# Attention and quantised feed-forward on one core: activation scales, normalising, the second quantiser's engine and all five orders changed

## The chip, the cores and the metric

The kernel runs on one core of a Trainium2 chip. The metric is the device time of one execution in microseconds; the time before is the median of three runs. The engines are TensorE (PE; PEld is its weight load), VectorE (DVE), ScalarE (ACT), GpSimd (POOL) and SyncE (SP), whose queue issues most DMAs. Each works through its own list of instructions in order and waits on semaphores for the others.

## The reference

One layer of cross attention with the 32 best keys of 1601, and one feed-forward part with quantised activations and ternary weights, for 2048 rows of 256 values:

```python
x = x + xattn(layernorm(x), ctx_1024, 32, Wq, bq, Wk, bk, Wv, bv, Wo, bo)
x = x + ffn(layernorm(x), w1, b1, w2, b2)

# xattn: scores = q @ k.T / 16; all but the 32 largest of a row are -inf; softmax; @ v; @ Wo.T + bo
def act_quant(x):
    scale = 127.0 / clip(max(abs(x), axis=-1), 1e-05)
    return clip(round(x * scale), -128, 127) / scale
def weight_quant(w):
    scale = 1.0 / clip(mean(abs(w)), 1e-05)
    return clip(round(w * scale), -1, 1) / scale
def bitlinear(x, w, b):                 # rmsnorm(x) = x * rsqrt(mean(x*x) + 1e-5)
    return act_quant(rmsnorm(x)) @ weight_quant(w).T + b
def ffn(x, w1, b1, w2, b2):             # 256 -> 1024 -> 256
    return bitlinear(gelu(bitlinear(x, w1, b1)), w2, b2)
```

## The kernel before

The 2048 rows are 16 tiles of 128 rows, two to a pair. The start turns the context, folds the query and key weights, makes keys and values in two parts of reduced precision (`high`, `low`), and makes the ternary weights. Then each tile t passes these steps, each named by a function with the engine in brackets:

- `ln1_stats` [DVE], `normalise_scale` and `normalise` [POOL], `turn_queries` [PE], `take_queries` [ACT], `split_queries` [POOL], for a pair j.
- `scores(t, c)` [PE] for four chunks c of about 400 keys, `copy_scores` [ACT] to `s_sb`, `candidates(t, c)` [DVE]: the 8 largest of each piece of 50.
- `best_8`, `next_8`, `count` [DVE] find the 32nd largest; `exp_all` [ACT]; `weigh` [DVE] zeroes in `e_all` what is below it. `turn_counts` [SP] brings the counts into one row, `largest_count` and `release` [DVE] branch on them and raise `p_ready`.
- `turn_weights(t, q)` [PE], `take_weights` [ACT], `weighted(t, q)` [PE] for four groups q; `residual` [POOL]; `attended` [DVE] makes x2; `moments` and `centre` [DVE] give its variance, the centred row and its maximum.
- `row_scales_1`, `quantise_1` [POOL], `turn_y1` [PE], `take_y1` [ACT], `up(t, h)` [PE] for two halves h, `hidden` [ACT], `add_bias` [POOL], `gelu`, `squares` [ACT], `gelu_max` [DVE].
- `row_scales_2` [POOL], `quantise_2` and `lower_2` [ACT], `turn_y2` [SP, a transposing DMA], `down` [PE], `keep_residual` [POOL], `output` [DVE], `store` [SP].

Rounding is by adding and subtracting `MAGIC` (12582912). In both scale functions on POOL seven tiny operations on 128x2 follow one another, each waiting for the last: mean square, its power -1/2, the product with the maximum, the step size, its reciprocal, the scale (step 5), and the factor of the product (step 6). In the last four tiles (12 to 15) the bias and parts of the second quantising go to DVE (`hidden`, `quantise_half`, `take_y2`), y2 is turned by TensorE, and tiles 14 and 15 have their scales one by one on DVE (`tile_spread_1`, `tile_scales`, `tile_spread_2`), with only the root on POOL (`root_1`, `root_2`). `hold_clock(23)` is 23 transposes with no use for the result.

The order of each engine is written by hand, as a list of calls at the end of its block, with a loop over rounds r in the middle: a round works on pairs r + 1, r, r - 1 and r - 2 in different steps. PSUM is eight banks, which `fill` gives out among a group and takes back by `drained`; `wait_full` and `wait_drained` are the waits that come with it.

## Time and profile before

| | us |
|---|---|
| median of 3 runs (lowest, highest) | 279.48 (278.39, 279.64) |
| the profiled execution, first to last instruction | 277.2 |
| TensorE busy | 262.5 (95%) |
| VectorE busy | 230.2 (83%) |
| ScalarE busy | 215.8 (78%) |
| GpSimd busy | 165.0 (60%) |
| mean granted TensorE clock | 0.999 |

The profiled execution's own time is known as its span alone, and the median of the runs lies 2.25 us above it. Busy time counts every moment in which at least one instruction of the engine runs, and matmul ends are modelled, so a busy TensorE can still have room. A wait is the idle time of an engine before an instruction, put down to the instruction that released it.

### The profile page before, as it was taken

The page shows a single profiled execution, that of the slowest core. Times are in us where ns is not written, and L with a number is a line of the kernel's source. Part 1 is how long each engine was busy: PE and PEld are TensorE (multiplying, and loading weights), DVE is VectorE, ACT ScalarE, POOL GpSimd, SP SyncE. Part 2 cuts the span into 40 slices and gives each one's busy share as a digit, 9 for nine tenths or more (in the row PEclk, how much of TensorE's full clock was granted, in tenths as well). Part 3 has the DMA queues.
Part 4 walks back from the last instruction along what each step waited for, and adds up shares of the span by engine and source line. Part 5 has one row for each costly group of instructions (what it writes and reads, how often), then busy time and mean ns, then how long its engine had stood idle before and what let it go on. Part 6 is the DMA issues. An engine that isn't in the chain of part 4 may idle for free. (4 is left out here: it accounts for less than half of the span.)

```text
span 277.2 us, 5366 instructions
## 1 busy us (share of the span) xinstructions
PE 262.5 (95%) x1527; PEld 230.4 (83%) x1527; DVE 230.2 (83%) x984; ACT 215.8 (78%) x323; POOL 165.0 (60%) x235
## 2 busy tenths in 40 slices
PE   7999999999999899999999999999999999799784
PEld 7999998998887788988898889888978898577463
DVE  2561868988979897989898989899989798989894
ACT  2567495586589988988799879987998899647762
POOL 3334409931888587849775887678767943612330
PEclk9999999999999999999999999999999999999999
DMA  6991010046000330025001500151004100610011
GB/s 223 316 342 40 4 38 0 1 79 151 2 2 0 77 78 0 0 69 125 0 4 45 139 5 4 38 140 18 0 1 124 31 1 2 151 38 5 0 38 38
DMA packets 29436, 16.42 MB, mean 59 GB/s; under 512 B 20445, under 2 KB 28190, under 8 KB 29406
## 3 DMA queue, kind: packets, MB, share of 16 engines
q1 hardware_dynamic: 28702, 15.02, 20.3%
q0 software_dynamic: 272, 0.79, 1.0%
q10 hardware_dynamic: 432, 0.26, 0.3%
q8 instruction: 12, 0.20, 0.3%
q14 instruction: 18, 0.15, 0.2%
HBM read 9.77 MB, written 2.10 MB: 43 GB/s over the span
## 5 line engine op out<-in xcount | busy, mean ns | idle before, releaser
L399 PE MATMUL bank<-vo,pT 128*128 128x257 f32 (+1 forms) x416 | 97.1, 381 | 2.4 <-ACT pT L1101 2.4
L399 PEld LDWEIGHTS bank<-vo,pT 128*128 128x128 f32 (+1 forms) x416 | 76.0, 190 | 15.1 <-ACT pT L1101 4.8
L1413 DVE MAX8 cand<-s_sb 128x8 f32<-128x50 f32 (+1 forms) x512 | 60.0, 201 | 1.6 <-issue 1.1
L258 PE MATMUL score<-k_high,q_low 128*128 128x400 f32 (+1 forms) x128 | 49.5, 387 | 0.0
L868 POOL TENSOR_TENSOR g<-g,b_bc 128x512 f32<-128x512 f32 x24 | 37.9, 1592 | 12.1 <-ACT g L1125 12.1
L258 PE MATMUL score<-k_low,q_high 128*128 128x400 f32 (+1 forms) x128 | 44.2, 346 | 0.0
L258 PE MATMUL score<-k_high,q_high 128*128 128x400 f32 (+1 forms) x128 | 44.0, 344 | 0.0
L1052 ACT ACTIVATE s_sb<-score 128x400 f32<-128x400 f32 x64 | 30.6, 504 | 10.2 <-PE score L258 10.1
L1101 ACT ACTIVATE pT<-bank 128x512 f32<-128x512 f32 x64 | 31.9, 514 | 4.2 <-PE bank L266 4.2
L1448 DVE SCALAR_TENSOR_TENSOR e_all<-s_sb,best,e_all 128x1601 f32<-128x1601 f32 x16 | 34.2, 2138 | 0.9 <-ACT e_all L1093 0.5
L266 PE MATMUL bank<-ident,e_all 128*128 128x128 f32 (+1 forms) x208 | 30.7, 273 | 2.6 <-ACT pT L1101 2.6
L1093 ACT ACTIVATE e_all<-s_sb,neg_max 128x1601 f32<-128x1601 f32 x16 | 26.1, 1629 | 4.5 <-DVE neg_max L1426 4.5
L266 PEld LDWEIGHTS bank<-ident,e_all 128*128 128x128 f32 (+1 forms) x208 | 24.4, 140 | 5.6 <-issue 3.6
L764 POOL TENSOR_SCALAR xn<-x_in,ln_mv,ln_r 128x256 f32<-128x256 f32 x16 | 27.8, 1741 | 0.9
L258 PEld LDWEIGHTS score<-k_high,q_low 128*128 128x128 f32 x128 | 24.1, 189 | 2.4
L258 PEld LDWEIGHTS score<-k_low,q_high 128*128 128x128 f32 x128 | 24.2, 189 | 0.7
L258 PEld LDWEIGHTS score<-k_high,q_high 128*128 128x128 f32 x128 | 24.1, 189 | 0.0
L1609 DVE TENSOR_REDUCE g_max<-g 128x1 f32<-128x1024 f32 x14 | 17.0, 1218 | 7.6 <-ACT g L1135 7.6
L1423 DVE MAX8 best<-cand 128x8 f32<-128x64 f32 (+1 forms) x64 | 20.8, 325 | 2.0
L822 POOL TENSOR_SCALAR row<-ln_mv 128x2 f32<-128x2 f32 x7 | 1.3, 192 | 28.8 <-issue 15.4
L1135 ACT ACTIVATE g<-g 128x1024 f32<-128x1024 f32 x14 | 14.9, 1067 | 3.7 <-POOL g L868 3.7
L1125 ACT ACTIVATE g<-bank,row 128x512 f32<-128x512 f32 x24 | 15.8, 685 | 2.3 <-PE bank L430 2.1
(162 smaller groups left out, 503.2 us busy)
## 6 DMA issues: line engine op xcount, KB each, us to landing
x_in<-in_x SPq DMA_DIRECT2D x16, 128.0 KB, 2.2
w_sb<-in_L_ffn_w SPq DMA_DIRECT2D x2, 1024.0 KB, 12.1
x_res<-in_x SPq DMA_DIRECT2D x16, 128.0 KB, 2.9
out<-o_sb SPq DMA_DIRECT2D x16, 128.0 KB, 2.0
ctx_sb<-in_ctx SPq DMA_DIRECT2D x2, 512.0 KB, 7.6
ctx_sb<-in_ctx SPq DMA_DIRECT2D x2, 256.0 KB, 4.1
b_bc<-in_L_ffn_b POOLq DMA_DIRECT2D x1, 512.0 KB, 7.6
w_q<-in_L_xattn_Wq SPq DMA_DIRECT2D x1, 256.0 KB, 2.8
```

The costliest lines, as they stand in the source:

```text
L258: ins = pe.matmul(out, a, b, start=(i == 0), stop=(i == len(steps) - 1))
L266: ins = pe.transpose(bank[0:src.shape[1], at:at + rows], src, ident[0:rows, 0:rows])
L399: ins = pe.matmul(bank[:, 0:DV], pT[0:n, t % 2, b * P:(b + 1) * P], vo[0:n, b, :], start=(b == 0), stop=(b == SB - 1))
L764: pool.tensor_scalar(xn[:, u, :], x_in[:, u, :], ln1_mv[:, u, 0:1], ln1_r[:, 1, u:u + 1], ALU.subtract, ALU.mult).then_inc(xn_ready, 1)
L868: pool.tensor_tensor(g[:, t % 2, part], g[:, t % 2, part], b1_bc[:, part], ALU.add).then_inc(biased, 1)
L1052: act.activation(s_sb[:, t % 2, at:at + n], score[c][:, 0:n], ACT.Copy).then_inc(s_copied, 1)
L1093: act.activation(e_all[:, t % 2, :], s_sb[:, t % 2, :], ACT.Exp, bias=neg_max[:, t % 2:t % 2 + 1], scale=SCALE).then_inc(e_ready, 1)
L1101: drain(act.activation(pT[0:rows, t % 2, lo * P:hi * P], bank(("p", t, q))[0:rows, 0:(hi - lo) * P], ACT.Copy), ("p", t, q))
L1413: ins = dve.max(cand[:, t % 2, k:CAND:PIECES], s_sb[:, t % 2, k * PIECE:end])
L1423: dve.max(best[:, u, k, :], cand[:, u, 0:DEPTH[k] * PIECES]).then_inc(topk_step[u], 1)
L1448: dve.scalar_tensor_tensor(e_all[:, u, :], s_sb[:, u, :], least_kept(t), e_all[:, u, :], ALU.is_ge, ALU.mult).then_inc(masked, 1)
L1609: dve.tensor_reduce(g_max[:, t % 2:t % 2 + 1], g[:, t % 2, :], AX.X, ALU.max, apply_absolute_value=True).then_inc(g_max_ready, 1)
```

## The change

- **Scales from the maxima alone.** Both activation scales are 127 over the largest value, in which the root mean square cancels. `scales_1` and `scales_2` make the step size from the maximum of the unnormalised row and its reciprocal, two operations; the clips become `CLIP1` and `CLIP2`. `quantise_1` and `quantise_2` need these two only. `dequant_1` and `dequant_2` make mean square, root and the factor of the product in four operations later on; they replace the rest of `row_scales_1` and `row_scales_2`. The same is done for tiles 14 and 15 on DVE (`tile_scales_1/2`, `tile_spread_1/2`, `tile_dequant_1/2`).
- **x normalised by add and multiply.** `normalise_scale` also makes the negated mean, and `normalise` adds it, where it subtracted the mean. Tiny operations with one function get a second one (times 1.0 or plus 0.0).
- **`quantise_2` and `lower_2` move from ACT to POOL**, as `tensor_scalar` over 1024 columns.
- **Orders.** All five lists of calls are written anew, without loops.

```diff
-ROW1, ROW2, X2S = 7, 7, 5
+ROW1, ROW2, X2S = 6, 6, 5
+CLIP1, CLIP2 = 1e-5 * EPS, 1e-5 * EPS ** 0.5
...
-                pool.tensor_scalar(xn[:, u, :], x_in[:, u, :], ln1_mv[:, u, 0:1], ln1_r[:, 1, u:u + 1],
-                                   ALU.subtract, ALU.mult).then_inc(xn_ready, 1)
+                pool.tensor_scalar(xn[:, u, :], x_in[:, u, :], ln1_r[:, 2, u:u + 1], ln1_r[:, 1, u:u + 1],
+                                   ALU.add, ALU.mult).then_inc(xn_ready, 1)
...
+            def quantise_2(t):
+
+                j = t // 2
+                pool.wait_ge(row2_step, j * ROW2 + 2)
+                if t >= 2:
+                    pool.wait_ge(y2_lowered, t - 1)
+                pool.tensor_scalar(y2_raised[:, t % 2, :], g[:, t % 2, :], row2[:, j % 2, 1, t % 2:t % 2 + 1], MAGIC,
+                                   ALU.mult, ALU.add).then_inc(y2_ready, 1)
+
+            def lower_2(t):
+
+                u = t % 2
+                pool.wait_ge(y2_ready, t + 1)
+                if t >= 2:
+                    pool.wait_ge(y2_turned[u], t // 2 * 16)
+                pool.tensor_scalar(y2[:, u, :], y2_raised[:, u, :], -MAGIC, 1.0, ALU.add, ALU.mult).then_inc(y2_lowered, 1)
...
+                pool.tensor_scalar(row1[:, v, 0, :], cen_max[:, pair], CLIP1, 1.0 / 127.0, ALU.max,
+                                   ALU.mult).then_inc(row1_step, 1)
+                pool.wait_ge(row1_step, base + 1)
+                pool.tensor_tensor(row1[:, v, 1, :], row1[:, v, 0, :], minus_one[:, :], ALU.pow).then_inc(row1_step, 1)
...
                 if t >= 2:
                     act.wait_ge(y2_ready, t - 1)
+                    act.wait_ge(g_sq_ready, t - 1)
...
-            def quantise_2(t):
-
-                j = t // 2
-                act.wait_ge(row2_step, j * ROW2 + 6)
-                if t >= 2:
-                    act.wait_ge(y2_lowered, t - 1)
-                act.activation(y2_raised[:, t % 2, :], g[:, t % 2, :], ACT.Identity, scale=row2[:, j % 2, 5, t % 2:t % 2 + 1],
-                               bias=magic_col[:, 0:1]).then_inc(y2_ready, 1)
...
             down(12)
-            up(15, 0)
-            up(15, 1)
             down(13)
-            hold_clock(23)
             turn_y2(14, 0)
...
             turn_y2(15, 0)
             turn_y2(15, 1)
-            down(14)
             down(15)
+            hold_clock(23)
```

The new orders, where the prediction speaks of them:

- DVE: `ln1_stats(0)` after `leave_context(2)`; `weight_means`, `candidates(0, 0)`, `ln1_stats(2)` before `leave_keys(3, *)`; then the rest of tile 0's candidates, its top-k, `weigh(0)`, `candidates(1, 0)`, (1, 1), `largest_count(0)`, `ln1_stats(3)`, `candidates(1, 2)`, `release(0)`, `candidates(1, 3)`. `attended(0)` after `weigh(2)`; `gelu_max(0)` and (1) amid the candidates of tile 5. After `release(15)`: `attended(14)`, `output(10)`, `moments(14)`, `hidden(12, *)`, `centre(14)`, scales and `quantise_1(14)`, `hidden(13, *)`, `gelu_max(12)`, (13), `output(11)`, `hidden(14, *)`, a maximum, `attended(15)`, ..., `quantise_1(15)`.
- PE: `scores(0, 0)`, (0, 1) after `project_keys(2, 1)`, then keys (3, *) with `weight_mean` between, one value block, the other scores of tile 0, scores of tile 1, the other values. In the tail `up(12)`, `up(13)` go between the turned weights of tile 15, `up(14)` into its weighted sums.
- ACT: `sum_weights(0)` after `take_keys(2, 0)`, `sum_weights(1)` before `copy_scores(0, 0)`.
- POOL: in each pair `scales_2`, `quantise_2`, `lower_2` of both tiles, then `scales_1` and `quantise_1` of the next pair, then `dequant_2`, `dequant_1`, `add_bias`.
- SP: `load_x(2)`, (3), (4) before `turn_counts(0)`, (1), (2).

## Rows read from the trace of the kernel before

**Rows 1.** Chain that ended last: start us, us, engine and line.

```profile
206.14 1.11 PE score L258 x6
207.24 0.87 PE bank L266 x8
208.12 0.87 PE bank L454 x8
209.86 3.48 PE bank L399 x16
...
216.08 0.45 PE bank L430 x2
```

**Rows 2.** Windows: length, busy us (count) per engine, PE clock, DMA share, GB/s.

```profile
47.28:247.10 199.82, 194.10 (x1094) 168.59 (x1093) 179.63 (x804) 168.78 (x245) 139.43 (x191) 1.00 0.20 46
...
124.47:152.61 28.14, 27.63 (x158) 23.90 (x156) 25.87 (x115) 25.35 (x37) 21.23 (x29) 1.00 0.19 46
...
266.00:272.00 6.00, 4.00 (x35) 3.50 (x34) 5.41 (x19) 4.04 (x7) 2.73 (x4) 1.00 0.08 25
```

**Rows 3.** Instructions of line 1448: ns minimum, median, maximum.

```profile
L1448 DVE SCALAR_TENSOR_TENSOR e_all<-s_sb,best,e_all x16: 1876/1886/2977, 37.2 to 244.2; 128x1601 f32<-128x1601 f32 x16
```

**Rows 4.** Timeline of DVE, the start: start us, us, [idle before, releaser].

```profile
27.86 0.64 DVE L1393 SCALAR_TENSOR_TENSOR k_low<-bank,k_bias,k_high 128x401 fp32r<-128x401 f32 x1 [5.18 <-ACT k_high L1033]
...
41.25 0.16 DVE L1404 TENSOR_SCALAR wmean<-bank 128x2 f32<-128x2 f32 x1 [1.66 <-PE bank L378]
...
42.80 3.69 DVE L1413 MAX8 cand<-s_sb 128x8 f32<-128x50 f32 x32 [1.13 <-issue]
...
47.28 0.19 DVE L1423 MAX8 best<-cand 128x8 f32<-128x64 f32 x1
```

**Rows 5.** Waits of DVE from 47.28 to 247.1: us, times, longest.

```profile
DVE g_max L1609 <- ACT g L1135: 7.6, 6, 1.9
DVE inv_sum L1497 <- PE bank L399: 5.1, 7, 1.0
```

**Rows 6.** Groups of DVE, 47.28 to 247.1 (mean ns), and timelines in tile 7.

```profile
L1448 DVE SCALAR_TENSOR_TENSOR e_all<-s_sb,best,e_all 128x1601 f32<-128x1601 f32 x15 | 32.3, 2155 | 0.9 <-ACT e_all L1093 0.5
...
L1455 DVE SCALAR_TENSOR_TENSOR cand_ge<-cand,best,cand_worth 128x256 bf16<-128x256 f32 x15 | 8.2, 545 | 0.5
...
132.97 2.97 DVE L1448 SCALAR_TENSOR_TENSOR e_all<-s_sb,best,e_all 128x1601 f32<-128x1601 f32 x1
...
132.99 1.27 POOL L868 TENSOR_TENSOR g<-g,b_bc 128x512 f32<-128x512 f32 x1 [0.91 <-ACT g L1125]
134.68 3.67 POOL L868 TENSOR_TENSOR g<-g,b_bc 128x512 f32<-128x512 f32 x2 [0.42 <-ACT g L1125]
```

**Rows 7.** Groups by shape, ACT: busy us, mean ns, idle before.

```profile
L1161 ACT ACTIVATE y_raised<-g,magic_col,row 128x1024 f32<-128x1024 f32 x14 | 17.3, 1242 | 0.2 <-POOL row L890 0.2
...
L1179 ACT ACTIVATE y<-y_raised,unmagic_col 128x1024 bf16<-128x1024 f32 x12 | 13.8, 1150 | 0.2
```

**Rows 8.** Groups by shape, POOL: busy us, mean ns, idle before.

```profile
L764 POOL TENSOR_SCALAR xn<-x_in,ln_mv,ln_r 128x256 f32<-128x256 f32 x16 | 27.8, 1741 | 0.9
...
L835 POOL TENSOR_SCALAR y<-cen,row 128x256 f32<-128x256 f32 x14 | 6.5, 479 | 0.7
...
L795 POOL TENSOR_SCALAR w_sb<-w_sb,winv 128x2048 f32<-128x2048 f32 x2 | 3.9, 1970 | 8.7 <-DVE winv L1406 8.7
```

**Rows 9.** Timelines of DVE and ACT in the tail.

```profile
246.63 0.26 DVE L1462 TENSOR_REDUCE doubtful<-counts_row 1x1 int32<-1x128 f32 x1
...
261.68 0.34 DVE L1556 TENSOR_SCALAR y<-cen,row 128x256 f32<-128x256 f32 x1
...
264.71 1.40 DVE L1584 SCALAR_TENSOR_TENSOR s_sb<-score,row,b_bc 128x512 f32<-128x512 f32 x2
...
270.48 0.82 ACT L1170 ACTIVATE y_raised<-s_sb,magic_col,row 128x512 f32<-128x512 f32 x1 [1.77 <-DVE row L1533]
...
274.51 0.48 DVE L1632 SCALAR_TENSOR_TENSOR o_sb<-score,row,x2b 128x256 f32<-128x256 f32 x1 [0.58 <-PE score L454]
```

More of the change, by code:

```diff
@@ L1729, in _ @@
[L1729 to L1730 removed]
+            candidates(1, 3)
+            best_8(1, 0)
+            next_8(1, 1)
+            next_8(1, 2)
+            next_8(1, 3)
+            count(1)
+            weigh(1)
+            largest_count(1)
+            candidates(2, 0)
+            release(1)
+            candidates(2, 1)
+            candidates(2, 2)
+            candidates(2, 3)
+            best_8(2, 0)
+            candidates(3, 0)
+            candidates(3, 1)
+            candidates(3, 2)
@@ new lines, in _ @@
+            gelu_max(0)
+            gelu_max(1)
+            candidates(5, 3)
+            best_8(5, 0)
+            attended(3)
+            centre(2)
+            next_8(5, 1)
+            moments(3)
+            next_8(5, 2)
+            centre(3)
+            next_8(5, 3)
+            count(5)
+            weigh(5)
+            largest_count(5)
+            attended(4)
+            release(5)
+            output(0)
+            moments(4)
+            candidates(6, 0)
+            candidates(6, 1)
@@ new lines, in _ @@
+            candidates(6, 2)
+            candidates(6, 3)
+            best_8(6, 0)
+            next_8(6, 1)
+            next_8(6, 2)
+            ln1_stats(5)
+            next_8(6, 3)
+            candidates(7, 0)
+            count(6)
+            gelu_max(2)
+            gelu_max(3)
+            output(1)
+            largest_count(6)
+            weigh(6)
+            release(6)
+            candidates(7, 1)
+            candidates(7, 2)
+            centre(4)
+            attended(5)
+            candidates(7, 3)
@@ new lines, in _ @@
+            centre(6)
+            next_8(8, 3)
+            gelu_max(4)
+            count(8)
+            output(2)
+            gelu_max(5)
+            candidates(9, 0)
+            ln1_stats(7)
+            weigh(8)
+            largest_count(8)
+            output(3)
+            release(8)
+            candidates(9, 1)
+            attended(7)
+            moments(7)
+            centre(7)
+            candidates(9, 2)
+            candidates(9, 3)
+            candidates(10, 0)
+            best_8(9, 0)
```

1386 lines of the change are left out of this document (900 added, 486 removed).

## The prediction, made before the changed kernel was timed

> **What bounds the kernel now.** I read the views in this order: the spacing of the matmuls in the chain, busy time by window, the timelines of the start, the waits of the vector engine (DVE), its groups, POOL beside it, the tail. The page has TensorE busy for 95% of the span, yet that is overlap, since ends are modelled: in the chain 16 matmuls of weights times values take 3.48 us, six of a score chunk 1.11, eight transposes 0.87, the eight of `down` 0.87, two of `up` 0.45 [rows 1]. A tile has 4 score chunks (4.44), 13 transposes (1.41), 13 weighted matmuls (2.83), 4 `up` (0.90), 8 `down` (0.87) and some 4 small turns (0.44): 10.9 us, 21.8 for a pair. A steady pair takes 28.14 us [rows 2], so TensorE has over 6 us of slack in it. In that window DVE is busy 25.87 us, ACT 25.35, POOL 21.23 [rows 2]. DVE's remainder is 1.4 us of named waits and 0.9 us of small gaps. DVE is the bound, ACT stands close behind, and part of DVE's busy time isn't work: `weigh` (L1448, the masking of `e_all`) takes 1.886 us at the median and up to 2.977 [rows 3].
>
> I cut DVE's time in three: until the first pick of the eight best of tile 1 (47.28 us [rows 4]); from there to the end of `largest_count(15)`, 246.63 + 0.26 = 246.9 us [rows 9], which frees the last tile's weights; and the tail to 277.2 us, 30.3 us long.
>
> **Part one, the start.** DVE stood idle 5.18 us before the keys (3, 0) while ACT took queries, values and the sum of w1; it waited 1.66 us for `weight_means` and 1.13 us after `release(0)` [rows 4]. The new orders put `ln1_stats(0)` some steps earlier, `scores(0, 0)` and (0, 1) ahead of the keys (3, *) and the first values, `weight_means` and `ln1_stats(2)` into the former gap, and candidates of tile 1 around `release(0)`. Stepped through with the present durations: ACT finishes keys (2, 0) near 20.5, both sums of weights and what stands between by 26.1, and copies score chunk (0, 0) by 26.6. TensorE issues without a pause here and only changes its order; chunk (0, 3) comes about 30.4, its candidates end near 32 against 34.1. Top-k of tile 0 (3.1) and `weigh(0)` (1.9) bring 37.0; tile 1's candidates (3.7), the largest count (0.3), `ln1_stats(3)` (0.94) and `release(0)` (0.4) bring the first pick of tile 1 to 42.3: 5.0 us earlier, with 0.94 us done ahead. I allow 41.5 to 44. On SP, `load_x(2)`, (3), (4) now stand ahead of `turn_counts(0)`, (1), (2), each waiting on `xn_ready`; the normalising they wait for lies over 5 us ahead of the count, so I cost them at nothing. Without that cover `largest_count` would wait, and `release` and the turned weights behind it.
>
> **Part two, the middle.** It lasted 246.9 - 47.28 = 199.6 us. Off it come:
> - the named waits, 7.6 (maxima after GELU) + 5.1 (`attended` after `weighted`) = 12.7 us [rows 5];
> - DVE standing behind POOL, 15 x (2.155 - 1.886) = 4.0 us of `weigh` and, by its undisturbed 0.48, 15 x (0.545 - 0.48) = 1.0 us of `count` [rows 3, 6];
> - work done elsewhere: ln1 of pair 3 (0.94), outputs 10 and 11 (0.95) and `hidden(12, 0)` (0.74), the last three now in the tail.
>
> That leaves 179.3 us. *Waits that return.* ACT loses `quantise_2` (1.24 us) in fourteen tiles and `lower_2` (1.15 us) in twelve [rows 7], 4.8 us of 25.35 in a pair. It relieves the engine that stands in front of both waits, but takes nothing off DVE. The orders also give slack: `attended(0)` stood after `count(1)`, now after `weigh(2)`; the maxima of tiles 0 and 1 stood in tile 4, now in tile 5. The last tiles keep less lag. I let 4 us of 12.7 return; 1 and 11 are the ends. The waits that are added (`hidden` for the squares, `lower_2` for the transposed y2) name things done a tile earlier: nothing. If `lower_2` did wait, `scales_1` and `quantise_1`, so y1, would be queued behind it on POOL.
>
> *POOL's own time.* `normalise` took 1.74 us at the mean for 256 columns with subtract and multiply, where `quantise_1` with multiply and add takes 0.479 for as many; multiply and add on 2048 columns take 1.97 us [rows 8]. A line through the two is 0.27 us + 0.83 ns a column. For add and multiply no row exists: the ends are 0.48 and the 1.23 us of an undisturbed `normalise`. I take 0.48, because it is the fast row's pair of operations in the other order; below that nothing is to be gained, since the time would be under the line of the fast form. The new operations of 1024 columns then cost 1.12 us each. A pair: 21.23 - 3.1 (x) - 0.4 (two small operations less in each of two sets, an estimate) + 0.2 (the negated mean) + 4.5 = 22.4 us of about 27. It fits into POOL's idle time and costs nothing by itself; without that cover y1 slips with it.
>
> *Standing behind POOL.* In tile 7 `weigh` starts at 132.97 and takes 2.97 us; POOL's add, started at 132.99, takes its plain 1.27; the next adds start within `weigh`, and two take 3.67 instead of 2.54 [rows 6]. DVE waited 1.08 us for the first, POOL for DVE after that. With POOL busier, and operations of 1.1 us where there was idle time, more starts of `weigh`, `count` and the centring meet one. From 5.0 us I go to 9.0; the ends are 5 (nothing changes) and 13 (15 x 0.87, near the worst row's 1.08 for every tile).
>
> The Trainium skill, SBUF — State Buffer, section Who interferes with whom, says that the ports which VectorE shares with GpSimd are locked for a whole instruction and that the order of issue decides who blocks; a VectorE operation with two SBUF inputs takes part. By that rule, the trace agrees (1.08 us of the add's 1.27), and it speaks against this change: if all 30 `weigh` and `count` met half an add, the term would be 19 us, and the time 276.
>
> Middle: 179.3 + 4 + 9 = 192.3 us; the last tile is released at 42.3 + 192.3 = 234.6 us.
>
> **Part three, the tail.** y1(15) was done at 262.0, hidden(15) began at 264.71, ACT's half of the quantising at 270.48, the last output ended at 274.99 [rows 9]. Between GELU (266.8) and 270.48 lay the squares, mean square, POOL's root, the maximum and four small steps. Scales need only the maxima now; three small steps of about 0.18 us remain. Stepping the new orders from the release R: ACT ends `gelu(12)` at R + 5.4; y1(14) is taken at 7.8, weighted(15) done at 9.9, `attended(15)` at 11.8, y1(15) at 17.2, since hidden (13) and (14), their maxima and two outputs stand before it; then 2.2 to hidden(15), 1.4, 0.65 GELU, 0.68 maximum, 0.55 scales, and `squares(15)` still ahead of ACT's half until 22.7, quantising 0.8, turn 0.6, taking 0.8, `down` 1.0, output 0.5: R + 26.4, and 2.2 for the store, 28.6. I take 29.0, against 30.3 with 1.7 us less work in it; ends 26.5 and 31. `hold_clock(23)` moves behind the last `down`: 23 x 0.109 = 2.5 us under the output and store (2.7), at no cost, and it no longer holds the clock for anything.
>
> **Sum.** 42.3 + 192.3 + 29.0 = 263.6 us of span. The median of the runs shown, 279.48, is 2.25 above the profiled span of 277.23; with the same addition the forecast is 266 us, 5% less.
>
> **Rivals.**
> - *DVE is fed throughout.* Locks stay at 5, 1 us of waits returns, tail 27: 42.3 + 179.3 + 6 + 27 + 2.25 = 257 us. For it: ACT is no longer near the bound. Against it: POOL is busier.
> - *The gain is handed back between DVE and POOL.* Locks 13, waits 9, start 43, tail 29: 43 + 179.3 + 22 + 29 + 2.25 = 275.5 us, 273 at half the excess. For it: quantising and lowering stand ahead of `scales_1` and `quantise_1` in POOL's queue, so a late maximum delays the next y1, and the locks as read above.
> - *Slower: add and multiply is no fast form on POOL.* A column then costs (1.23 - 0.27)/256 = 3.7 ns, `lower_2` 4.1 us, and `normalise` stays. POOL's 139.4 us of the middle [rows 2] are, by the forecast, 27 more (24 x 1.12), 19 less for x, 6 less for scales and for a ternary step that goes ahead: 141. Here come 35 + 6 on top, and some 15 blocked behind DVE: 197, more than DVE's 192. From 4 us a lowering POOL is the bound; its bursts of 10 us make y1 and GELU late, 10 us of waits come back, R is 250, and with a tail of 31 the time is 283 us.
> - *The clock falls in the tail*, with the hold gone. 266:272 was granted 1.00 [rows 2], 2.4 GHz. At 1.2 GHz the last turns, `up` and `down`, about 2.6 us of the path, double: 268.5 us, in the forecast's own range.
>
> **How the numbers follow.** Forecast, 261 to 269.5: 0.53, the clock case within. Fed throughout, 254 to 261: 0.20. Handed back, 269.5 to 278: 0.18. Slow POOL form: 0.06. Another cause of slower: 0.03. The range, 256 to 275, leaves out 0.06 below and 0.14 above. A measurement of this kernel tells some 0.5% from no change (278.1 to 280.9). Faster by more: 0.53 + 0.20 + 0.16 = 0.89; within: 0.04; slower: 0.07.
>
> **What would show it.** `normalise` at 0.5 us and POOL's operations on `y_raised` and `y` at 1.1; ACT under 190 us busy; first pick of tile 1 near 42 us; DVE's named waits in the middle near 4 us; `weigh` at a mean over 2.2 us; the last release near 235 us and 29 us behind it. Wrong would be a pair that still takes 28 us, POOL over 85% busy, or `lower_2` at 4 us.

## The result and the profile after

| | before | after |
|---|---|---|
| median of the runs, us | 279.39 | 283.49 (281.81 to 285.84) |
| ratio, 95% interval | | 1.0165 (1.0109 to 1.0220) |
| profiled execution's own time, us | | 282.66 |
| its span, us | 277.2 | 280.9 |

The change makes the kernel 1.65% slower. The forecast was 266.0 us, 5% faster. The busy times on the page of the changed kernel:

```profile
PE 262.0 (93%) x1527; PEld 230.1 (82%) x1527; DVE 232.4 (83%) x978; ACT 188.3 (67%) x297; POOL 182.5 (65%) x255
```

ACT lost 27.5 us of work and POOL gained 17.5, as planned, while VectorE's busy time didn't fall but rose by 2.2 us. The best way to see where the time went is to cut both executions at the same pieces of work. I take the first `best_8` of tiles 1, 8 and 14, and ask for busy time by window. First the kernel before, then the changed one (length, busy us and count per engine, clock, DMA share, GB/s):

```profile
47.28:142.20 94.92, 92.48 (x514) 80.91 (x513) 84.18 (x390) 77.17 (x113) 67.60 (x86) 1.00 0.19 43
142.20:226.10 83.90, 82.71 (x474) 72.24 (x473) 75.89 (x339) 76.07 (x112) 63.02 (x86) 1.00 0.19 45
226.10:277.20 51.10, 41.60 (x257) 33.03 (x255) 42.55 (x137) 34.52 (x51) 15.31 (x33) 1.00 0.14 37
```

```profile
42.71:142.60 99.89, 93.75 (x528) 81.79 (x527) 83.91 (x387) 65.35 (x105) 62.43 (x86) 1.00 0.18 39
142.60:226.50 83.90, 81.98 (x468) 71.88 (x466) 76.47 (x335) 61.43 (x98) 67.37 (x88) 1.00 0.20 44
226.50:280.90 54.40, 46.07 (x282) 37.40 (x280) 43.39 (x133) 34.24 (x52) 30.02 (x42) 0.97 0.13 34
```

The start is 4.6 us shorter. The stretch to tile 8 is 5.0 us longer, and with that the whole gain of the start is gone. Three pairs in the steady state take 83.9 us in both kernels, to the tenth, although ScalarE (ACT) has 14.6 us less to do in them. The end is 3.3 us longer. -4.6 + 5.0 + 0 + 3.3 = +3.7 us, the difference of the spans. In the stretch to tile 8, VectorE works 84 us in both kernels and is idle 16.0 us instead of 10.7.

VectorE's waits between 42.71 and 248.74 us (us, times, longest), which answer to [rows 5]:

```profile
DVE cand L1743 <- ACT s_sb L1293: 7.5, 8, 2.0
DVE inv_sum L1827 <- PE bank L400: 6.3, 7, 1.4
DVE o_sb L1976 <- POOL row L1071: 2.9, 1, 2.9
DVE cand L1743 <- issue: 1.0, 2, 0.6
DVE cand L1743 <- DVE doubtful L1792: 1.0, 1, 1.0
DVE g_max L1953 <- ACT g L1379: 1.0, 2, 0.7
```

With three smaller ones they add up to 21.0 us. The wait for GELU went from 7.6 to 1.0 us. In its place VectorE waits 7.5 us for scores, and 6.3 for weighted values. TensorE works through its list in order, and in this stretch it stood at `turn_y1` for POOL:

```profile
PE bank L267 <- POOL y L1015: 5.5, 4, 1.8
```

Scores that stand behind such a place in the list come later; that this is the whole reason for the 7.5 us is not shown (e1, below, took most of these waits away and was slower). Two of the four places, in TensorE's timeline (start, length, then in brackets the idle time before and its releaser):

```profile
78.13 0.66 PE L267 MATMUL bank<-ident,y 128*128 128x128 f32 x4 [1.62 <-POOL y L1015]
...
104.97 0.66 PE L267 MATMUL bank<-ident,y 128*128 128x128 f32 x4 [1.13 <-POOL y L1015]
```

Why y1 is late at 104.97 can be read in VectorE's and POOL's timelines:

```profile
101.24 2.88 DVE L1778 SCALAR_TENSOR_TENSOR e_all<-s_sb,best,e_all 128x1601 f32<-128x1601 f32 x1
```

```profile
101.14 1.30 POOL L926 TENSOR_TENSOR q_low<-q_full,q_high 128x512 fp32r<-128x512 f32 x1
102.53 2.39 POOL L1015 TENSOR_SCALAR y<-cen,row 128x256 f32<-128x256 f32 x2
```

`weigh` starts 0.1 us after POOL's subtraction and takes 2.88 us instead of 1.89; the two `quantise_1`, 0.48 us each when nothing stands in the way, are issued while it runs and end at 104.92, 0.8 us after `weigh` does. This is the lock of [rows 6], now with a third engine behind it: TensorE's 1.13 us.

A part of the loss is in the clock, and the profiled execution doesn't show all of it. The four executions of the changed kernel had mean granted clocks of 0.994, 0.994, 0.988 and 0.982, and spans of 280.9, 280.0, 282.5 and 284.0 us. The kernel before, measured beside the other runs, had 0.991 to 1.000 and 276.4 to 279.0. What one fall costs can be read where the same work ran with it and without: the changed kernel, and then a4, which differs from it in the tail alone. Both have the same 1.77 us of waiting for y1 in front of 136 us.

```profile
134.00:136.00 2.00, 0.28 (x3) 0.28 (x4) 1.97 (x7) 0.00 (x0) 2.00 (x3) 1.00 0.04 0
136.00:138.00 2.00, 2.00 (x14) 1.68 (x13) 1.93 (x11) 1.18 (x2) 1.65 (x5) 1.00 0.23 58
```

```profile
134.00:136.00 2.00, 0.23 (x2) 0.09 (x2) 2.00 (x6) 0.00 (x0) 2.00 (x3) 0.98 0.04 0
136.00:138.00 2.00, 2.00 (x8) 1.99 (x9) 1.89 (x12) 0.69 (x1) 1.65 (x5) 0.50 0.16 31
```

In a4 the clock fell to 0.50 there, the lower of its two levels (1.2 GHz, where 1.00 is 2.4 GHz), and from the pick of tile 7 to that of tile 8 it took 15.85 us instead of 14.27: 1.6 us. So a wait of TensorE for POOL can be paid twice, and the second time not in every execution.

### The profile page after: what moved, and what is told of

Same layout as the page of the kernel before. It is cut to its first block, busy times and chain, and to the rows that moved or that the text cites. A ratio compares the mean times of both kernels' runs of the same rounds, so it can differ in the third digit from the quotient of the medians.

```text
span 280.9 us, 5388 instructions
## 1 busy us (share of the span) xinstructions
PE 262.0 (93%) x1527; PEld 230.1 (82%) x1527; DVE 232.4 (83%) x978; ACT 188.3 (67%) x297; POOL 182.5 (65%) x255
## 4 chain that ended last, share of the span: by engine, by line
PE 46%; POOL 18%; DVE 17%; issue 10%; ACT 5%; DMA 3%; DVEq 1%; SPq 0%; POOLq 0%; ACTq 0%
PE score L259 13%; PE bank L400 12%; PE bank L259 7%; PE bank L267 6%; POOL y L1015 4%; POOL g L1048 3%; DVE cand L1743 3%; DMA ctx_sb<-in_ctx 3%; DVE g_max L1953 2%; PE bank L431 2%; POOL y_raised L964 2%; ACT g L1379 2%; POOL row L993 1%; DVE e_all L1778 1%; PE bank L455 1%
## 5 line engine op out<-in xcount | busy, mean ns | idle before, releaser
L1743 DVE MAX8 cand<-s_sb 128x8 f32<-128x50 f32 (+1 forms) x512 | 61.6, 202 | 9.9 <-ACT s_sb L1293 7.5
L1293 ACT ACTIVATE s_sb<-score 128x400 f32<-128x400 f32 x64 | 31.5, 505 | 17.0 <-PE score L259 16.6
L1048 POOL TENSOR_TENSOR g<-g,b_bc 128x512 f32<-128x512 f32 x24 | 35.3, 1476 | 8.4 <-ACT g L1369 8.3
L1778 DVE SCALAR_TENSOR_TENSOR e_all<-s_sb,best,e_all 128x1601 f32<-128x1601 f32 x16 | 33.8, 2115 | 0.0
L964 POOL TENSOR_SCALAR y_raised<-g,row 128x1024 f32<-128x1024 f32 x14 | 17.4, 1246 | 0.6
L926 POOL TENSOR_TENSOR q_low<-q_full,q_high 128x512 fp32r<-128x512 f32 x8 | 10.2, 1279 | 10.6 <-ACT q_full L1285 10.6
```

The source lines that it names most:

```text
L964: pool.tensor_scalar(y2_raised[:, t % 2, :], g[:, t % 2, :], row2[:, j % 2, 1, t % 2:t % 2 + 1], MAGIC, ALU.mult, ALU.add).then_inc(y2_rea ...
L1048: pool.tensor_tensor(g[:, t % 2, part], g[:, t % 2, part], b1_bc[:, part], ALU.add).then_inc(biased, 1)
L1293: act.activation(s_sb[:, t % 2, at:at + n], score[c][:, 0:n], ACT.Copy).then_inc(s_copied, 1)
L1743: ins = dve.max(cand[:, t % 2, k:CAND:PIECES], s_sb[:, t % 2, k * PIECE:end])
L1778: dve.scalar_tensor_tensor(e_all[:, u, :], s_sb[:, u, :], least_kept(t), e_all[:, u, :], ALU.is_ge, ALU.mult).then_inc(masked, 1)
```

## The experiments

All ratios are to the kernel before, measured on the same chip beside each run; 0.01 is 2.8 us. "Old orders" are the five lists of before, "new orders" those of the changed kernel.

| kernel | us | ratio (95%) |
|---|---|---|
| a1 old orders, new arithmetic | 284.36 | 1.0162 (1.0136 to 1.0188) |
| a2 old orders, quantising on ScalarE | 276.77 | 0.9882 (0.9858 to 0.9906) |
| a3 new orders, quantising on ScalarE | 314.21 | 1.1216 (1.1192 to 1.1240) |
| a4 changed kernel, holder moved | 282.56 | 1.0092 (1.0062 to 1.0122) |
| b1 new orders, POOL quantises 32 columns | 279.21 | 0.9978 (0.9956 to 0.9999) |
| b2 as a3, spread | 308.99 | 1.1034 (1.1010 to 1.1058) |
| b3 as a2, new start | 277.94 | 0.9923 (0.9899 to 0.9946) |
| b4 old orders, POOL quantises 32 columns | 276.79 | 0.9881 (0.9858 to 0.9904) |
| c1 before, two of three score products | 278.37 | 0.9961 (0.9938 to 0.9983) |
| c2 changed kernel, two of three | 283.41 | 1.0161 (1.0113 to 1.0209) |
| c3 as a2, two of three | 274.49 | 0.9835 (0.9797 to 0.9873) |
| c4 as b3, two of three | 274.91 | 0.9832 (0.9802 to 0.9863) |
| e1 changed kernel, later turns | 286.88 | 1.0268 (1.0239 to 1.0298) |
| e4 as a2, waits moved | 277.91 | 0.9947 (0.9924 to 0.9971) |
| e5 as e4, shorter tail | 277.58 | 0.9935 (0.9909 to 0.9962) |
| f1 as e4, two of three | 276.28 | 0.9895 (0.9852 to 0.9938) |
| f2 as b1, two of three | 278.34 | 0.9954 (0.9923 to 0.9985) |
| f3 as a2, shorter tail | 276.47 | 0.9891 (0.9848 to 0.9933) |

### The arithmetic and the orders apart: a1, a2, a3, b2

**a1** takes the changed kernel and puts the five lists of before under it, with the new calls at the places of the old:

```diff
-                    row_scales_2(r + 2)
+                    scales_2(r + 2)
+                    quantise_2(2 * r + 4)
+                    lower_2(2 * r + 4)
+                    quantise_2(2 * r + 5)
+                    lower_2(2 * r + 5)
+                    dequant_2(r + 2)
```

> All of the new arithmetic (scales from the maxima alone, x normalised by add and multiply, the second quantised activations and their lowering on GpSimd), under the five orders of the kernel before; the clock holder stands where it stood before. Theory O (the new orders cost the time: in the new order of TensorE the turns of y1 stand ahead of scores and come before GpSimd has them, and everything behind them slips): the first pick of tile 1 is back at 47 us, the middle from there to the last release falls below the 199.6 us of before, since g_max and the scales no longer wait for ScalarE, and the time is 270 to 278 us. Theory G (quantising and lowering on GpSimd, 2.4 us a tile, lengthens the way to y1 under any order, and the locks with VectorE add to it): the 5 us of the earlier start are lost and nothing comes back for them, 285 to 290 us.

**a2** leaves the quantising where it was:

```diff
-                pool.tensor_scalar(y2_raised[:, t % 2, :], g[:, t % 2, :], row2[:, j % 2, 1, t % 2:t % 2 + 1], MAGIC,
-                                   ALU.mult, ALU.add).then_inc(y2_ready, 1)
+                act.activation(y2_raised[:, t % 2, :], g[:, t % 2, :], ACT.Identity, scale=row2[:, j % 2, 1, t % 2:t % 2 + 1],
+                               bias=magic_col[:, 0:1]).then_inc(y2_ready, 1)
```

> The same, but the second activations are quantised and lowered by ScalarE, at their old places in its order; only the scales and the normalising are new. Theory O: 273 to 279 us, as the old orders hold the time whoever quantises; within 2 us of the kernel with old orders and quantising on GpSimd. Theory G: 275 to 279 us too, but that kernel is slower than this one by 6 us or more.

Measured 284.4 and 276.8 us. The new orders, taken whole, are worth nothing against the old ones under the new arithmetic (1.0165 and 1.0162), and the quantising on POOL costs 7.6 us under the old orders: theory G, whose difference was 6 us or more, though a1 itself lies just under its 285 us. The new scales and the new `normalise` gain 1.2%. Cut at the same picks, a1 takes 46.4 + 97.2 + 87.3 + 51.0 us and a2 47.3 + 94.0 + 83.8 + 49.8: most of the price of the POOL quantising falls before tile 14, 3.2 and 3.4 us. The groups of VectorE in a1 and then in a2 (busy us, mean ns) show what it consists of:

```profile
L1542 DVE TENSOR_SCALAR cen<-x,ln_mv 128x256 f32<-128x256 f32 x16 | 9.8, 615 | 0.3
L1483 DVE SCALAR_TENSOR_TENSOR cand_ge<-cand,best,cand_worth 128x256 bf16<-128x256 f32 x16 | 9.6, 598 | 0.5
...
L1651 DVE TENSOR_REDUCE g_max<-g 128x1 f32<-128x1024 f32 x14 | 17.0, 1218 | 10.1 <-ACT g L1193 10.1
```

```profile
L1537 DVE TENSOR_SCALAR cen<-x,ln_mv 128x256 f32<-128x256 f32 x16 | 5.5, 345 | 0.3
L1478 DVE SCALAR_TENSOR_TENSOR cand_ge<-cand,best,cand_worth 128x256 bf16<-128x256 f32 x16 | 8.0, 503 | 0.5
...
L1646 DVE TENSOR_REDUCE g_max<-g 128x1 f32<-128x1024 f32 x14 | 17.0, 1218 | 7.7 <-ACT g L1158 7.7
```

VectorE is busy 233.1 us in a1 and 227.7 in a2, 5.4 more. The centring has 4.3 us more and the count 1.6, standing behind POOL, and `weigh` 0.5 less; another 2.4 us are the longer wait for GELU. 5.4 + 2.4 = 7.8 us, against 7.0 us between the spans.

**a3** is the other half, the new orders with the quantising back on ScalarE, each pair ahead of the next `take_y1`; **b2** is the same with each pair where ScalarE had room in the trace of the changed kernel.

```diff
+            quantise_2(0)
+            lower_2(0)
+            quantise_2(1)
+            lower_2(1)
             take_y1(1)
```

> The changed kernel with its new orders, but the second activations quantised and lowered by ScalarE, the pair of them just ahead of the next take_y1 in ScalarE's order. Theory G: GpSimd reaches y1 2.4 us a tile earlier, TensorE no longer waits at the turns of y1, ScalarE has 26 us a run more to do but was busy 188 of 281 us: 274 to 279 us. Theory O: the waits stay, at other places, 282 to 288 us.

> New orders, quantising on ScalarE, but each pair placed where the trace of the changed kernel shows ScalarE idle or just done with the squares, some 15 us earlier than in the kernel of 314 us, where SyncE's turns of the activations stood ahead of the counts' and VectorE waited 26 us for them. If that queue was the whole of the 314 us: 276 to 282 us. If the new orders do not bear a later y2 at all: over 290 us. Faster than the changed kernel only if GpSimd's share (theory G) outweighs what ScalarE's 29 us push back.

Measured 314 and 309 us. Both theories missed for a3; of the two cases for b2 the one over 290 us came. VectorE's largest waits, a3 and then b2:

```profile
DVE doubtful L1792 <- DMA counts_row<-counts: 26.4, 6, 9.8
```

```profile
DVE doubtful L1792 <- DMA counts_row<-counts: 13.4, 4, 6.3
DVE cand L1743 <- ACT s_sb L1250: 13.0, 6, 4.5
```

SyncE's list has `turn_y2` of a pair ahead of `turn_counts`, so a late y2 keeps VectorE from its counts, and `release` with it. The new lists bear neither of these two placings on ScalarE. The two runs say nothing on what POOL's quantising costs under them; b1 does.

### What each engine's work is worth: b1, b4

Both leave out part of the result: POOL quantises and lowers 32 of 1024 columns of tiles 0 to 11.

```diff
-                pool.tensor_scalar(y2_raised[:, t % 2, :], g[:, t % 2, :], row2[:, j % 2, 1, t % 2:t % 2 + 1], MAGIC,
+                n = F if t >= LAST - 2 else 32
+                pool.tensor_scalar(y2_raised[:, t % 2, 0:n], g[:, t % 2, 0:n], row2[:, j % 2, 1, t % 2:t % 2 + 1], MAGIC,
```

> The changed kernel, in which GpSimd quantises and lowers only 32 of the 1024 columns of tiles 0 to 11; every instruction, wait and place stays (the rest of those columns isn't computed). It takes 12 x (1.12 + 1.04) us, less some 0.2 us each for the stubs, about 22 us of work off GpSimd, and nearly all of its locks with VectorE. Theory G (the length of this work on GpSimd and its locks cost the time): the middle falls from 206.0 us to 192 to 197, the whole to 269 to 275 us. Theory O (the new orders by themselves): 280 to 283 us, as only the locks, at most 4 us, go.

> Old orders with all of the new arithmetic (284.4 us), and the same stubs of 32 columns on GpSimd for tiles 0 to 11. Against the kernel with old orders and quantising on ScalarE (276.8 us) it has ScalarE's 29 us of quantising taken away and next to nothing put in its place: what that relief is worth by itself. Theory G1 (ScalarE stands in nobody's way): 276 to 277 us. Theory G2 (my forecast: the waits for ScalarE's gelu, 7.7 us in that kernel, fall with the relief): 269 to 273 us.

b4 has next to nothing of the quantising on any engine (the stubs, and tiles 12 and 13 on POOL) and takes 276.79 us; a2 has it on ScalarE and takes 276.77. **Relieving ScalarE of 28.7 us of work is worth nothing** in these orders, and the whole 7.6 us of a1 are POOL's doing. VectorE's waits for GELU and for the weighted values are the same in both, a2 first:

```profile
DVE g_max L1646 <- ACT g L1158: 7.7, 6, 1.9
DVE inv_sum L1520 <- PE bank L400: 5.1, 7, 1.0
```

```profile
DVE g_max L1652 <- ACT g L1194: 7.7, 6, 1.9
DVE inv_sum L1526 <- PE bank L400: 5.4, 7, 1.0
```

b1 is 1.9% below the changed kernel, 5.2 us by the ratios and 4.3 by the medians, with VectorE busy 228.4 instead of 232.4 us. It is between the theories: POOL's quantising costs 4 to 5 us under the new orders too, and what is left, 279.2 us, is 2.4 us slower than b4 in spite of the earlier start.

### The start by itself: b3

a2 with the head of the five lists from the changed kernel, up to the first pick of tile 1 (one of the moves):

```diff
-            project_keys(3, 0)
-            project_keys(3, 1)
             scores(0, 0)
             scores(0, 1)
+            project_keys(3, 0)
+            weight_mean()
+            project_keys(3, 1)
+            project_values(0)
             scores(0, 2)
```

> Old orders with quantising on ScalarE (276.8 us), and the start of all five lists laid as in the changed kernel, up to the first pick of tile 1. That pick moves from 47.3 to 42.7 us. If the start is a gain of its own: 271.5 to 273 us. If the middle gives it back (the rounds are paced by the chain through y1, gelu and y2, and not by VectorE's list): 275 to 277 us.

The pick of tile 1 comes at 42.09 us, 5.2 earlier, and the time is 1.2 us longer, above both ranges. VectorE's timeline shows the whole gain lost before the next tile, whose first pick came at 59.0 us in a2:

```profile
42.09 0.23 DVE L1753 MAX8 best<-cand 128x8 f32<-128x64 f32 x1
...
51.87 0.17 DVE L1827 RECIPROCAL inv_sum<-bank 128x1 f32<-128x1 f32 x1 [6.61 <-PE bank L400]
...
59.23 0.23 DVE L1753 MAX8 best<-cand 128x8 f32<-128x64 f32 x1
```

VectorE waits 6.61 us for the weighted sums of tile 0, which need every block of the projected values; those were put behind the scores to make the start shorter. TensorE had 40.3 us of work done at 42.1, against 45.7 at 47.3, so it owed 5 us. In the changed kernel the same debt is paid later: its picks of tiles 2 to 5 come at 52.4, 63.2, 75.1 and 94.5 us, against 59.0, 72.3, 85.6 and 100.4 before. It is 10.5 us ahead at tile 4 and 0.4 behind at tile 8 (142.6 against 142.2). Up to the pick of tile 4, before and then changed:

```profile
0.00:85.61 85.61, 83.64 (x495) 78.06 (x495) 61.52 (x283) 54.49 (x88) 43.67 (x59) 1.00 0.33 97
0.00:75.12 75.12, 72.59 (x442) 69.20 (x443) 57.00 (x280) 46.72 (x77) 30.71 (x55) 1.00 0.39 114
```

TensorE has 11 us less work done at that point, and VectorE 4.5: the lead is work put off. b3 leaves `attended(0)` at its old place, where the changed kernel moved it behind `weigh(2)`; the start together with that move alone was not run.

### Is TensorE the bound? c1 to c4

Each score chunk leaves out one of its three products, so the scores are less exact:

```diff
-                steps = [(a, b) for ah, al, bh, bl in factors for a, b in ((al, bh), (ah, bl), (ah, bh))]
+                steps = [(a, b) for ah, al, bh, bl in factors for a, b in ((al, bh), (ah, bl), (ah, bh))[first:]]
```

> The kernel before, with one of the three products of each score chunk left out (low queries by high keys), so that its scores are less exact: 64 x 2 matmuls of 0.185 us, 23.7 us of TensorE's work, some 21 of it behind the first pick of tile 1. Nothing of any other engine changes. Theory T (TensorE paces the middle: 26 matmuls of weights by values a tile, not 13, make 27.4 of the 28.14 us of a pair): the time falls until VectorE's 25.9 us of a pair are the bound, 1.5 to 2 us a pair, to 264 to 270 us. Theory D (VectorE is the bound and TensorE has 6 us of slack, as I forecast): 278 to 280 us.

> The changed kernel with the same product left out. Theory T: TensorE has room for its waits on GpSimd's y1 (5.5 us), and the start of 42.7 us counts: 264 to 274 us. Theory D: the 21 us of VectorE's waits in the middle come from GpSimd and the queues and stay, 280 to 284 us.

> Old orders, new scales and normalising, quantising on ScalarE (276.8 us), with the same product left out. Theory T: 262 to 268 us, 1 to 3 below the kernel before with that product left out, since VectorE is now next and has 1 to 2 us less of locks. Theory D: 275 to 277 us.

> The same with the start laid anew (277.9 us with all three products). Theory T: the start of 42.1 instead of 47.3 us was paid back by TensorE work that it put off (5.3 us); with TensorE relieved, VectorE's earlier start counts, and this kernel is 3 to 5 us faster than the one with the old start. Theory D: the same 0 to 1 us slower as with all products, the round's latency deciding.

Theory T falls. TensorE's busy time drops by 17.0 us in c1, 15.9 in c2 and 19.8 in c3. The kernel before gains 0.4%, the changed one nothing (1.0161 against 1.0165), and a2 1.3 us by the ratios, 2.3 by the medians and 3.1 by the mean spans, no more than the 3.3 us by which its first pick of tile 1 came earlier (44.0 us). c4 and c3 are equal, so the earlier start doesn't pay with a relieved TensorE either. Three steady pairs of c3, and VectorE's waits in them:

```profile
137.70:221.00 83.30, 75.29 (x426) 63.57 (x426) 75.26 (x338) 75.55 (x112) 52.79 (x82) 1.00 0.19 45
```

```profile
DVE g_max L1646 <- ACT g L1158: 3.2, 3, 1.9
DVE inv_sum L1520 <- PE bank L400: 2.1, 3, 0.7
```

TensorE works 7.7 us less than in a2's 83.8 us, and the pairs are 0.5 us shorter. The two waits, 3.2 and 2.1 us, are those of the kernel before in the same pairs. TensorE's own new idle time goes into waiting for ScalarE: 3.7 us for turned weights in these pairs, and in the whole of c1 the transposes of the weights wait 12.6 us for it where they waited 2.6. With less to do TensorE also had a lower clock (means of 0.981 to 0.994 in the executions of c1, against 0.991 to 1.000 in those of the kernel before), but that doesn't hide a gain: of c3's executions the one at 1.000 had a span of 272.1 us and those at 0.993 had 270.8 and 271.2.

### Places or latency: e1, e4, e5, f1, f2, f3

**e1** moves three `turn_y1` behind the work that follows them, and `dequant_2(0)` ahead of `scales_1(1)`:

```diff
             scores(6, 0)
-            turn_y1(1)
             down(0)
             scores(6, 1)
+            turn_y1(1)
```

> The changed kernel, with three turns of y1 put behind the work that follows them in TensorE's order (pairs 0, 1 and 2, where it stood 5.5 us for GpSimd in all), and dequant_2(0) ahead of scales_1(1) on GpSimd, since VectorE's first output stood 2.9 us for it. Theory P (the gain of the start is lost in the places where one engine's list stands for another's, between tiles 4 and 8): 277 to 280 us. Theory L (what comes late is the chain centring, scales, y1, up, GELU itself, which no place in a list shortens): 282.5 to 284 us, the waits reappearing behind up and GELU.

286.9 us, 1.0% slower than the changed kernel. TensorE's waits for y1 fell from 5.5 to 1.6 us, and VectorE then waited 4.4 us in one place for `down`, and TensorE 3.3 us for the low queries, behind which the granted clock was 0.50 from 106 to 108 us; in the profile of the changed kernel it was 1.00 there. Theory P is refuted for these moves, and the size of L as well: a step that is moved off one wait stands before another.

**e4** moves two steps of VectorE's list behind candidates:

```diff
-                if live(r - 1):
-                    gelu_max(2 * r - 2)
                 if live(r + 1):
                     candidates(2 * r + 2, 1)
+                if live(r - 1):
+                    gelu_max(2 * r - 2)
...
                 if live(r):
+                    candidates(2 * r + 3, 0)
                     attended(2 * r + 1)
```

> Old orders, new scales and normalising, quantising on ScalarE (276.8 us), with two moves in VectorE's list of each round: the first candidates of the next tile go ahead of attended, and those of the even tile ahead of the first maximum after GELU, about 1 us of work each. Its named waits in the middle are 7.7 (maxima) and 5.1 us (attended). Neither less work on TensorE nor on ScalarE shortened them. Theory P (they are a matter of the place in VectorE's list): they fall to under 4 us, and the time to 267 to 271 us. Theory L (a loop of fixed latency runs through them): the waits keep their sum within 3 us, at these places or others, and the time stays at 275.5 to 278 us.

277.9 us, 1.1 us slower than a2. The waits for GELU and the weighted values fell from 12.8 to 2.7 us, and 11.8 us of new ones stand before the candidates. In the three steady pairs:

```profile
DVE cand L1436 <- ACT s_sb L1072: 2.1, 2, 1.1
DVE g_max L1646 <- ACT g L1158: 1.9, 1, 1.9
DVE cand L1436 <- issue: 1.6, 3, 0.5
```

5.6 us, against 5.3 in c3 and in the kernel before. Of the 11.8 us, 8.2 are waits for ScalarE's copies of the scores. ScalarE was relieved in b4 alone, at the old places; e4 with ScalarE relieved was not run. **e5** is e4 with a shorter tail, and is compared with e4; **f3** is a2 with that tail alone. On ScalarE `squares(15)` goes behind its half of tile 14, and on VectorE:

```diff
             tile_scales_2(14)
+            quantise_half(14, 1)
             tile_spread_2(14)
-            output(13)
             gelu_max_half(15, 0)
             gelu_max_half(15, 1)
-            quantise_half(14, 1)
             tile_scales_2(15)
             quantise_half(15, 1)
-            tile_dequant_2(14)
+            output(13)
             tile_spread_2(15)
             take_y2(14, 1)
+            tile_dequant_2(14)
```

> The same kernel of 276.8 us with its tail laid so that nothing of tile 14 stands between the last GELU and the quantising of tile 15: scales_2(14) and both halves of its quantising ahead of the last maxima, output(13) behind the last quantising. Scales of tile 15 end 0.5 us and ScalarE's half starts 0.5 us earlier: 0.4 to 1.2 us faster if VectorE's steps set the end. No change if TensorE's turn of tile 14 behind the holder's matmuls does.

> The kernel of 276.8 us with the shorter tail alone. The run that was to show the tail carried the two moves of VectorE's list too, by my mistake; against the kernel with the moves alone it was 0.3 us faster, its last stretch 0.5 us shorter. Here 275.9 to 276.6 us; if the tail brings nothing, 276.8.

e5 is 0.3 us below e4 and f3 0.3 us below a2, both within their intervals. f3 is the lowest of the exact kernels by its median, 276.5 us, but not to be told from a2.

**f1** puts e4 and the left-out product together, **f2** b1 and the left-out product; their edits stand above.

> Old orders, new scales and normalising, quantising on ScalarE, the two moves in VectorE's list, and one of the three products of each score chunk left out (less exact scores, 23.7 us less for TensorE). Each by itself did little: the product left out gave 274.5 us against 276.8, with the 12.9 us of waits for GELU and the weighted values as before; the moves gave 277.9 us, with those waits turned into 8.2 us for copied scores. Theory B (two bounds at one height: VectorE's list with its waits, and TensorE's 27.4 us of a pair of 28.14; whoever is relieved alone meets the other): both together free the 10 us that neither did, 263 to 268 us. Theory L (a loop of fixed latency whatever the engines do): 273 to 276 us.

> The changed kernel with GpSimd quantising 32 of 1024 columns of tiles 0 to 11 (279.2 us with three products) and two of the three products of each score chunk. By itself the product left out gave 283.4 us against 283.5. Theory B for the new orders: with GpSimd and TensorE both relieved, VectorE's work of 228 us paces, 266 to 272 us. Theory L: the waits of the new orders stay (y1, released weights, low queries, each late for TensorE), 277 to 280 us.

Theory B falls as well: 276.3 and 278.3 us, the first just above the range of theory L. Three steady pairs of f1:

```profile
139.60:223.90 84.30, 76.83 (x426) 63.15 (x426) 77.46 (x339) 75.38 (x111) 52.53 (x82) 1.00 0.19 45
```

VectorE's waits there are 2.1, 1.6 and 0.7 us, 4.4 in all, but it is busy 77.5 us instead of 75.3 in c3: `weigh` takes 2306 ns at the mean over the kernel, against 2109 in c3, and `count` 619 against 526. What the moves took out of the waits came back as standing behind POOL. Three steady pairs last 83.3 to 84.4 us in before, changed kernel, a2, b4, c3, e4 and f1, with ScalarE at 61 or 76 us, TensorE at 75 to 83, and the waits at different places. Off this mark are a1 with 87.3 us and b1 with 82.0, where POOL's load under the same orders was changed, and a3 and b2 (97.6 and 94.0), where y2 came late.

Two explanations are left. One is a ring of dependences through all four engines. The other is VectorE's own list: it is busy 74 to 77 us of every such stretch, and what is left over is 8.0 us in before, 7.4 in the changed kernel, 8.1 in a2 and e4, 8.0 in c3 and 7.9 in b1 (6.8 in f1, 10.5 in a1). No run took work off VectorE, so none decides between the two, and which ring it would be is not shown either.

### The tail: a4

```diff
             down(14)
+            hold_clock(23)
             turn_y2(15, 0)
             turn_y2(15, 1)
             down(15)
-            hold_clock(23)
```

> The changed kernel, with the 23 matmuls that hold TensorE's clock moved from the end of its queue to between down(14) and the turn of the last activations. Both theories: they ran alone for 2.5 us after the last output and ended last, that tail goes; down(15) took 1.9 us at a granted clock of 0.56 to 0.59 and may now take 1.0: 1.3 to 3.5 us faster than the changed kernel, 279.5 to 282 us. If the holder delays the turn it stands before, the gain is under 1 us.

1.0092 against 1.0165: 0.7%, 2.0 us faster than the changed kernel by the ratios, a gain within the 1.3 to 3.5 us expected, though the time itself is above the range given. The two intervals together leave room for 0.3 to 3.8 us, and the medians differ by 0.9. Against a1 (1.0162, with a narrower interval) it is 0.7% too: the new orders with this holder are worth about 2 us over the old ones. Windows and TensorE's timeline in the tail of the changed kernel, and then the last `down` of a4:

```profile
270.00:273.00 3.00, 0.63 (x6) 0.32 (x4) 2.84 (x8) 2.68 (x5) 0.00 (x0) 1.00 0.00 0
273.00:275.00 2.00, 1.09 (x8) 0.86 (x8) 1.12 (x5) 1.19 (x2) 0.55 (x1) 1.00 0.19 66
275.00:277.00 2.00, 1.41 (x7) 1.02 (x8) 0.49 (x1) 0.04 (x1) 0.00 (x0) 0.56 0.03 8
277.00:279.00 2.00, 2.00 (x13) 1.96 (x11) 0.48 (x1) 0.00 (x0) 0.00 (x0) 0.59 0.02 8
```

```profile
275.59 1.86 PE L455 MATMUL score<-w2T,y2T 128*128 128x256 bf16 x8 [0.90 <-ACT y2T L1244]
277.25 3.36 PE L421 MATMUL bank<-ident 128*128 128x128 f32 x23
```

```profile
277.50 1.03 PE L455 MATMUL score<-w2T,y2T 128*128 128x256 bf16 x8 [0.90 <-ACT y2T L1244]
```

TensorE was busy 0.63 of 3 us, and the granted clock then fell to 0.56, that is to the lower level of 1.2 GHz for most of the window. The last `down` took 1.86 us instead of 1.03, and the holder, which now follows it, ran 3.36 us, until 280.61, 2.5 us behind the end of the last output (278.07). With the holder in the gap the clock is 1.00 there, and both prices go. They are smaller than they look. `down` gives back 0.8 us. The store of the last output takes as long as most of the holder: in a4 the output ends at 279.16 and the span at 281.4, 2.2 us later, and 278.07 + 2.2 = 280.3 against 280.9, so the holder itself costs 0.6. The profiled span of a4 is no shorter than that of the changed kernel because of the fall at 136 us; its one execution with a mean clock of 0.999 had a span of 279.3 us.

## Why the prediction was wrong, point by point

- **Part one** held: first pick of tile 1 at 42.71 us against 42.3. But it was booked as a gain of the whole. It is a loan: b3 and c4 show that an earlier pick is worth nothing with `attended(0)` at its old place, as the values that TensorE put off are owed to it, and in the changed kernel the lead of 10.5 us at tile 4 went with 11 us of TensorE's work put off.
- **TensorE's slack**, "over 6 us" in a pair, was a miscount. A tile has 26 records of `weighted` and not 13: 416 in 16 tiles, two for each of 13 blocks. 26 x 3.48 / 16 = 5.66 us instead of 2.83 [rows 1], which makes 13.7 us a tile and 27.4 of the 28.14 us of a pair. The page's 95% was right. A forecast of 263.6 us of span held 262.5 us of TensorE work and should have been stopped by that. The miscount was not the whole cause, though: with 17 to 20 us less work on TensorE (c1, c3), the forecast's gain still doesn't come.
- **The waits that return** are the step that failed most. 12.7 us of waits were taken off, because the engine in front of them was relieved and the orders gave slack, and 4 put back; 21.0 came. The middle took 206.0 us (42.71 to 248.74) and not 192.3, 13.7 more, and this term alone is 17.0 of it; with 21.0 and the 9.8 of the next point in it, the sum would be 210.1, and 4.1 us of small gaps and small steps went the other way. b4 shows the first reason to be void: with ScalarE relieved of the whole, the waits for GELU and for weighted values are the same to 0.3 us. So ScalarE's load did not set them; what does stays open. Subtracting named waits from a stretch is not a forecast, unless what releases them is shown to come earlier.
- **Standing behind POOL.** The forecast was 5 us before and 9 after; 9.8 came by the same reckoning: 3.7 us in `weigh` (2115 ns against 1886), 1.8 in `count`, and 4.3 in the centring, which I named as joining and gave no number. The total is right. In the middle VectorE's busy time rose less, from 179.6 to 180.2 us, as 2.6 us of its work went elsewhere by the forecast's own list. A faster `normalise` takes little of the standing away: in a2 `weigh` stays at 2114 ns against 2138, and `count` goes from 541 to 503, 1.0 us in all over the kernel. The forecast also took the locks as VectorE's cost alone; 101.24 to 104.97 us shows them reach TensorE through y1. By the Trainium skill, SBUF — State Buffer, section Who interferes with whom, a `tensor_scalar` of VectorE can take the shared port pair too, when it runs in a two-port mode; the trace agrees (the centring goes from 355 ns at most before to 1367 ns at most after), and this should have been in the sum.
- **Prices on POOL** were near: `quantise_2` 1.25 us at the mean, `lower_2` 1.16, with a forecast of 1.12; `normalise` 0.65 with the locks, forecast 0.48. The groups (busy us, mean ns, idle before):

```profile
L964 POOL TENSOR_SCALAR y_raised<-g,row 128x1024 f32<-128x1024 f32 x14 | 17.4, 1246 | 0.6
L973 POOL TENSOR_SCALAR y<-y_raised 128x1024 bf16<-128x1024 f32 x12 | 14.0, 1163 | 0.9
L1015 POOL TENSOR_SCALAR y<-cen,row 128x256 f32<-128x256 f32 x14 | 12.8, 922 | 0.7
...
L920 POOL TENSOR_SCALAR xn<-x_in,ln_r 128x256 f32<-128x256 f32 x16 | 10.3, 648 | 4.5 <-PE bank L267 4.3
```

  "It fits into POOL's idle time and costs nothing by itself" was the second step to fail: b1 puts the price at 4 to 5 us and a1 against b4 at 7.6, with POOL busy only 65% of the span. `quantise_1`, which makes y1, went from 0.48 to 0.92 us at the mean.
- **Part three**: 29.0 us forecast, 32.2 measured (248.74 to 280.9). `quantise_1(15)` was done 18.6 us after the release, hidden(15) began 20.5 after it and ScalarE's half 24.0, each 1.1 to 1.4 us later than stepped through. The holder "at no cost" and a clock that stays were wrong: 2.0 us by a4, of which the traces show 1.4. The rival on the clock had the mechanism for the tail and about the size, 2.6 us, but of other parts: `down` lost 0.8 us where turns, `up` and `down` were to lose 2.6, and it lacked the holder behind the last output and the falls in the middle.
- **The addition** of 2.25 us compares a median with the span of one execution. The changed kernel's profiled execution has 282.66 - 280.9 = 1.8; this is small beside the rest.
- **The rivals.** The slower one named a POOL form that proved fast. "Handed back between DVE and POOL" had the mechanism, late y1 behind POOL's queue and locks of 13 us, but kept the credit of the start and 3.7 us of the waits, and so ended at 275.5.
- **The signs.** Of what was to show the forecast, the first pick, ScalarE under 190 us (188.3) and, nearly, the prices on POOL came. The waits (21.0 us and not 4), the last release (248.7 and not 235) and `weigh` over 2.2 us (2.115) did not. Of what was to show it wrong, one came: a pair still takes 28 us (83.9 / 3).

## What to carry to other kernels

Before a named wait is booked as a gain, ask what would make its releaser earlier, and relieve the engine in front of the wait in an experiment first: here 29 us off ScalarE were worth nothing, and 17 to 20 us off TensorE between nothing and 3. Measure an earlier start by the work that each engine has done at that point, not by the time of one step. Count the records of each group against its total (416 / 16) before you set a busy share of 95% aside. Work given to GpSimd was paid here by VectorE, and by whoever waits for GpSimd's short steps, though GpSimd is idle a third of the time.

## What was not expected of the hardware

- On POOL, the same 256 columns of `normalise` took 1.74 us at the mean with subtract and multiply [rows 8], and 0.65 with add and multiply; undisturbed 1.23 and, in a2, 0.55 us.
- VectorE's `tensor_scalar` with one tensor in SBUF stands behind POOL: the centring's mean went from 345 to 615 ns when POOL quantised, with the same order on VectorE (a2, a1).
- The granted clock stayed at 1.00 through 3 us in which TensorE was busy 0.63, and was 0.56 in the window from 275 on, when the work had come back. It cost after the gap, not in it.
- After the same 1.77 us of TensorE waiting, the granted clock from 136 to 138 us was 1.00 in one execution (the changed kernel) and 0.50 in another (a4), and 1.6 us went with it.
